# Pre-norm attention layer (delta-rule RNN) with ReLU FFN on 8 cores: four sets of eight PSUM copies each become one VectorE instruction

## The reference

```
q = silu(x @ Wq); k = silu(x @ Wk); v = silu(x @ Wv)
f = x @ Wf1 @ Wf2; log_f = log_sigmoid(f)
beta = sigmoid(x @ Wbeta) * 2.0
k = l2norm(k); k_ = -beta * k
gk = interleave(log_f, 0); a = interleave(k_ * exp(log_f), k_); bb = interleave(k, k)
kk = interleave(0, k); vv = interleave(0, v); qq = interleave(0, q)
def step(S, inp):
    bS = b_t @ S
    S = exp(g) * S + a_t (x) bS + k_t (x) v_t
    o = q_t @ S
y = o[odd steps] * sigmoid(x @ Wog1 @ Wog2)
y = y / sqrt(mean(y*y over the head) + EPS) * norm_w
attn = y @ Wo
x = x + attn(layernorm(x))
x = x + (relu(layernorm(x) @ w1 + b1) @ w2 + b2)
```

## Time and profile before

| | us |
|---|---|
| median of 2 runs of the kernel before | 6550.92 (6539.94 and 6561.9) |
| the profiled execution, its own time | 6540.92 |
| its span (first to last instruction, slowest core) | 6539.3 |
| spans of the eight cores | 6481.3 to 6539.3 |

### The profile page before, as it was taken

One profiled execution on the slowest core, in us unless ns is written; L12 is line 12 of the kernel. 1 busy time (PEld: TensorE's weight loads), 2 busy tenths in 40 slices (PEclk: granted clock), 3 DMA queues, 4 the chain that ended last, 5 costly groups with the idle time before them and its releaser, 6 DMA issues.

```text
span 6539.3 us, 88394 instructions; the slowest of 8 cores (6481.3 to 6539.3 us)
## 1 busy us (share of the span) xinstructions
PE 4050.7 (62%) x30717; PEld 2720.6 (42%) x30797; DVE 2399.2 (37%) x5555; ACT 1899.4 (29%) x3443; POOL 458.3 (7%) x456
## 2 busy tenths in 40 slices
PE   0066566665656565666565666656565648788888
PEld 0034344443434343434343433434353425555555
DVE  0144435353535353534344343435353511111111
ACT  0042333233332323232323233333323212222222
POOL 0010101010100000010101010101000000000000
PEclk9976666676766676676766666666666768888898
DMA  9511010101010101010110101010101030000000
GB/s 106 123 46 42 24 46 20 46 20 46 20 65 1 65 1 65 1 65 7 59 33 33 46 20 46 20 46 20 62 4 46 1 126 33 30 27 27 27 27 26
DMA packets 92522, 255.96 MB, mean 39 GB/s; under 512 B 11531, under 2 KB 14252, under 8 KB 89270
## 3 DMA queue, kind: packets, MB, share of 16 engines
q1 hardware_dynamic: 91382, 229.33, 10.4%
q0 software_dynamic: 704, 20.97, 2.9%
HBM read 233.48 MB, written 58.72 MB: 45 GB/s over the span
## 4 chain that ended last, share of the span: by engine, by line
PE 48%; DVE 20%; ACT 11%; issue 9%; DMA 6%; another core or an unknown queue 3%; POOL 2%; SPq 1%; DVEq 1%; ACTq 0%; POOLq 0%
PE PB L84 48%; DVE Pm_sb L84 6%; DVE X_sb L84 3%; DVE Lam L84 2%; ACT U_sb L84 2%; DVE lncol L84 2%; DMA Wbuf<-wbf_Wk 2%; ACT v_bf L84 1%; DVE yT_bf L84 1%; ACT L84 1%; SPq L84 1%; DVE scrA L84 1%; DMA x_sb<-x2scratch 1%; ACT yT_bf L84 1%
## 5 line engine op out<-in xcount | busy, mean ns | idle before, releaser
L84 ACT CAST U_sb<-PB 128x512 bf16<-128x512 f32 x1024 | 600.0, 586 | 1387.3 <-PE PB L84 1347.3
L84 DVE CAST X_sb<-PB 128x512 bf16<-128x512 f32 x640 | 439.2, 686 | 639.5 <-PE PB L84 639.5
L84 PE MATMUL PB<-U_sb,consts 128*128 128x128 bf16 x3584 | 597.3, 253 | 104.8 <-ACT U_sb L84 104.8
L84 PE MATMUL PB<-U_sb,Pm_sb 128*128 128x128 bf16 x3584 | 591.1, 254 | 42.9 <-DVE Pm_sb L84 40.7
L84 DVE CAST Pm_sb<-PB 128x512 bf16<-128x512 f32 x768 | 518.8, 683 | 172.3 <-PE PB L84 172.3
L84 PE MATMUL PB<-consts,yT_bf 128*128 128x128 bf16 x640 | 76.5, 294 | 709.0 <-DVE yT_bf L84 638.1
L84 PE MATMUL PB<-X_sb,Pm_sb 128*128 128x128 bf16 x2048 | 220.9, 237 | 416.9 <-DVE Pm_sb L84 416.9
L84 PEld LDWEIGHTS PB<-U_sb,consts 128*128 128x128 bf16 x3584 | 412.7, 115 | 134.9 <-issue 125.3
L84 PE MATMUL PB<-W_bf,hfm 128*128 128x512 bf16 x2000 | 443.1, 381 | 17.7 <-ACT hfm L84 15.9
L84 PEld LDWEIGHTS PB<-U_sb,Pm_sb 128*128 128x128 bf16 x3584 | 414.1, 116 | 64.0 <-issue 61.5
L84 PEld LDWEIGHTS PB<-consts,yT_bf 128*128 128x128 bf16 x640 | 58.4, 132 | 727.6 <-issue 727.6
(11 more groups left out here) (142 smaller groups left out, 6858.8 us busy)
## 6 DMA issues: line engine op xcount, KB each, us to landing
Wbuf<-wbf_Wv SPq DMA_DIRECT2D x128, 256.0 KB, 7.5
Wbuf<-wbf_Wo SPq DMA_DIRECT2D x128, 256.0 KB, 4.7
Wbuf<-wbf_Wq SPq DMA_DIRECT2D x15, 2048.0 KB, 7.9
Wbuf<-wbf_Wk SPq DMA_DIRECT2D x120, 256.0 KB, 5.9
wbf_w<-w POOLq DMA_DIRECT2D x2, 8192.0 KB, 81.5
x_sb<-x SPq DMA_DIRECT2D x32, 512.0 KB, 3.9
x2scratch<-x_sb SPq DMA_DIRECT2D x32, 512.0 KB, 2.9
W_bf<-wbf_w SPq DMA_DIRECT2D x64, 256.0 KB, 5.7
```

The costliest lines, as they stand in the source:

```text
L84: inst = getattr(e, fname)(*args, **kw)
```

## The change

In three places the eight copies of `pe_transpose_8` become one `tensor_copy` of 128x1024 (64x1024 for Ktm): Atm, Ktm, and lnT in phase A, where a permuted access pattern (`_perm_in`, `_perm_out`) orders the eight blocks. The eight multiplications by nw_col ahead of Wo become one `tensor_tensor` with nw_col broadcast. Phase B's copies stay as they are. The lists that are dealt into the levels get 14 instructions shorter (32, nper = 5).

```
 def pe_transpose_8(src_fn, dst_fn, tsrc, tdst, pbank, tpbank, n=8,
-                   rows=128):
+                   rows=128, dst_batched=None):
...
+    if dst_batched is not None:
+        out_ap, in_ap = dst_batched
+        b.op("V", "tensor_copy", out_ap, in_ap,
+             reads=[tpbank], writes=[tdst])
+        return
...
+def _perm_in(pbank):
+    return pbank[:].bitcast(BF16).rearrange(
+        "p (s k e) -> p k s e", s=2, k=4)
+def _perm_out(dst, grp):
+    return dst[:, grp * 1024:(grp + 1) * 1024].rearrange(
+        "p (k s e) -> p k s e", k=4, s=2)
...
-                    lambda i: lnT[:, idx[i][0] * MACRO + idx[i][1] * 128:
-                                  idx[i][0] * MACRO + (idx[i][1] + 1) * 128],
-                    tyT, tlnT, pbank, tpbank)
+                    None, tyT, tlnT, pbank, tpbank,
+                    dst_batched=(_perm_out(lnT, grp), _perm_in(pbank)))
...
-                            lambda i: Atm[:, i * 128:(i + 1) * 128],
-                            tAm, tAtm, pb, tpb)
+                            None, tAm, tAtm, pb, tpb,
+                            dst_batched=(Atm[:], pb[:].bitcast(BF16)))
...
-                            lambda i: Ktm[:, i * 128:(i + 1) * 128],
-                            tKt, tKtm, pb2, tpb2, rows=64)
+                            None, tKt, tKtm, pb2, tpb2, rows=64,
+                            dst_batched=(Ktm[:], pb2[:].bitcast(BF16)[0:64, :]))
...
-                        for i in range(8):
-                            kk, sub = idx[i]
-                            b.op("V", "tensor_scalar_mul",
-                                 q_bf[:, kk * MACRO + sub * 128:
-                                      kk * MACRO + (sub + 1) * 128],
-                                 pbank[:].bitcast(BF16)[:, i * 128:(i + 1) * 128],
-                                 nw_col[:, kk:kk + 1],
-                                 reads=[tpbank, tnw], writes=[tq], inc=(i == 7))
...
+                        nw4 = nwb[:, grp * 4:(grp + 1) * 4]
+                        nw_b = nw4.rearrange("p (k o) -> p k o", o=1)
+                        nw_b = nw_b.unsqueeze(2).broadcast_to((128, 4, 2, 128)) \
...
+                        b.op("V", "tensor_tensor", _perm_out(q_bf, grp),
+                             _perm_in(pbank), nw_b, ALU.mult,
+                             reads=[tpbank, tnw], writes=[tq])
```

More of the change, by code:

```diff
@@ L968, in build_program @@
                                  inc=(i == 7))
-                        for i in range(8):
-                            kk, sub = idx[i]
-                            b.op("V", "tensor_scalar_mul",
-                                 q_bf[:, kk * MACRO + sub * 128:
-                                      kk * MACRO + (sub + 1) * 128],
-                                 pbank[:].bitcast(BF16)[:, i * 128:(i + 1) * 128],
-                                 nw_col[:, kk:kk + 1],
-                                 reads=[tpbank, tnw], writes=[tq], inc=(i == 7))
+                        nwb = bass.AP(nw_col.handle if hasattr(nw_col, "handle")
+                                      else nw_col, 0, [[8, 128], [1, 8]]) \
+                            if False else nw_col[:]
+                        nw4 = nwb[:, grp * 4:(grp + 1) * 4]
+                        nw_b = nw4.rearrange("p (k o) -> p k o", o=1)
+                        nw_b = nw_b.unsqueeze(2).broadcast_to((128, 4, 2, 128)) \
+                            if hasattr(nw_b, "unsqueeze") else nw_b
+                        b.op("V", "tensor_tensor", _perm_out(q_bf, grp),
+                             _perm_in(pbank), nw_b, ALU.mult,
+                             reads=[tpbank, tnw], writes=[tq])
                     for sub in range(NSUB):
```

## The result

| | us |
|---|---|
| before, median of 10 runs | 6539.0 (6519.75 to 6607.27) |
| changed kernel, median of 11 runs | 6643.6 (6632.97 to 6775.05) |
| ratio | 1.0154, 95% interval 1.0118 to 1.0189 |

The account below looks back on a forecast made before the run. Waits between engines, in a closed DVE-PE ring of doubling levels, were taken to bound the kernel. From 6540.9 us, +120 for the 48 chunks with a next one and -31 for the gains made 6630 us, range 6560 to 6690.

Parts of the forecast that it names:

- The moved wait: Level 2: PE queues behind a transpose waiting for the second Am product; 1.66 us more at full clock, 3.15 at half.
- Which clock: Level 2 after the new wait: PE at half clock in nine levels of ten, making 3.0 us a chunk.
- Level 3: Five transposes in front instead of one: idle falls from 2.4 to about 1.8 us, gain 0.5 us a chunk.
- levels 3 and 4 became slower: Sign of a wrong forecast; level 3 was expected near 1.8 us and level 4 to change by 0.
- The batched copies: A batched copy takes 0.68 us, q_bf 1225 ns; lnT gains 15 us in all, q_bf 13 us.
- The small term of chunk 0: Atm and Ktm copies ahead of T_sb in chunk 0: 0.2 us each time, 3 us in all, bounds 0 and 15.
- The hidden copies: Atm and Ktm copies in chunks 1 to 3 fall into DVE's idle stretch, hidden by PE and casts; gain 0.
- The sum: 6540.9 + 120 - 31 = 6630 us, 1.4% more than the profiled execution, 1.2% above the median of the two runs shown.
- Gains alone: Rival: the Am wait costs nothing, so 6510 us, perhaps 6490 with level 3; chance 0.06.
- the slow batch: Rival: the batched copy takes 1.22 us in place of 0.68, giving 6650 us; chance 0.07.
- full clock at the wait: Rival: PE at full clock in level 2 behind the Am wait, giving 6566 us; chance 0.10.
- slow clock throughout: Rival: half clock through levels 2 to 4 of 48 chunks, up to 4.9 us a chunk, 6747 us; chance 0.09.

Follow-up runs that it names:

- f3: The changed kernel with 34 filler products on PE ahead of the transpose that waits for Am in level 2; 6661.9 us, ratio 1.0126 to the kernel before.
- a2: Eight copies each as in the kernel before, but dealt to the levels as in the changed kernel; 6745.4 us, ratio 1.0308.
- a3: Changed kernel with Am products still behind level 1's casts, but the first transpose one level later; 6527.7 us, ratio 1.0008 to the kernel before.
- b1: Changed kernel's batched copies, list dealt 7, 7, 7, 7, 4, so Am products stand early and seven transposes precede level 2; 6538.9 us, ratio 0.9992.
- f1: b1 plus filler products nobody reads on PE, making up seven instructions with the transposes ahead of levels 1 to 4; 6374.2 us, ratio 0.9755.
- f4: f1 plus 24 fillers ahead of the HQ products, 4 ahead of levels 5 and 6, 10 ahead of the output products; 6284.9 us, ratio 0.9485.

## Why the prediction was right, point by point

**The sign and the size.** 6630 us was forecast and 6643.6 measured; against the kernel before of the same runs that is +1.5% where +1.2 to 1.4% was said.

**The moved wait** was right in mechanism and size. Worked out were 4.90 us between the casts at half clock and 3.41 at full clock; 4.85 was measured (f3, mostly at full clock: 3.66). Am ended 1.39 us behind the cast where 1.40 was said. a2 has the order without the batching and the loss, a3 has the late Am without the waiting transpose and no loss: the cause is the transpose queued on PE ahead of work that is ready.

**Which clock.** Nine in ten at half clock were taken; it was all of them (19 of 6144 U products of level 2 ran at full clock). This made the term 48 x 3.1 = 148 us in place of 144.

**Level 3** is the term that was wrong. The prediction gave it 0.5 us a chunk for its five transposes ("if five transposes do what seven do"), 24 us in all. Measured was 2.36 us, 0.1 more than before, with 0.52 of these levels at half clock where 0.36 were. That "levels 3 and 4 became slower" was one of the prediction's own signs of being wrong, and both did, by 0.1 us each (level 4 from 2.04 to 2.12). f3 shows what was missing: with the same five transposes, but PE busy through the wait of level 2, level 3 took 1.86 us. What PE had done before counts too, not only the transposes right in front. In level 3 those in front make no visible difference: six of them (b1) give 2.21 us, one of them (before) 2.26.

**The batched copies** were right: 683 to 692 ns (0.68), 1225 ns (1.225), lnT 0.91 us a macro tile (0.92), q_bf 0.84 (0.82). The small term of chunk 0 (0.2 us) was wrong: T_sb starts 0.3 us earlier, but nothing behind it does, so it is worth nothing.

**The hidden copies** were costed at nothing, and their DVE time was indeed hidden. Not seen was the tail: the changed deal puts five transposes ahead of level 5 and one ahead of level 6, where three and none stood, and the tail is 0.3 us shorter in each of the three chunks. The copies are not the cause, since a2, which has the same places and eight copies each, has 8.51 us too; in all deals without fillers the tail goes with the transposes ahead of levels 5 and 6 (8.5 to 8.6 us with five and one, 8.9 with three and none, 9.2 with none). The time is saved in the output products behind level 6 (5.5 us from the first to the last in place of 5.8); level 6's own U products were at full clock before too. f1 has 8.62 us with none of these transposes, so here as well what PE did earlier counts.

**The sum.** In the traces: level 2 +148 us (144 forecast), the other levels +13 (-24), the tail -16 (0), lnT and q_bf -28 (-28), chunk 0 nothing (-3): 117 us, where the forecast had 89. The two terms of the clock's kind were off by 37 and by 16 us and cancelled in part; that the total came out as close is to that extent luck.

**The rivals.** Gains alone was refuted by PE's wait for Am; the slow batch by the 683 ns; full clock at the wait by the traces (none of the U products of level 2); slow clock throughout by levels 3 and 4, which came to 2.36 and 2.12 and not to 2.97 us.

## What to carry to other kernels

When instructions are dealt into a pipeline by count, making the list shorter moves every one of them: look at what stands first in each slot, and never put an instruction that waits in front of independent work on an in-order engine. A merge of small copies is worth only what someone waits for, here two places of four. And before tuning the order, look at what TensorE did in the microseconds ahead of each burst: idle work there can be worth more (5% here) than the instructions saved.

## What the runs showed that I had not expected

Moving transposes that cost nobody any time changes the time of the products behind them, by 0.4 us in level 2 (1.76 us with seven in front, 2.18 with one). In this chain with many short idle times PE did the U products of a third of the levels 1 and 3 at 1.2 GHz, and nearly all at 2.4 GHz once fillers stood in the idle times (f1). Filler products in the idle times raised the slowest core's granted clock over the span from 0.736 to 0.816 (f4), and took 5% off the time. Phase B, where PE is busy for 80% of the time at a granted clock of 0.87 (kernel before, 5300 to 6500 us), had no fillers; whether they would pay there was not tried. How many fillers are needed at the least was not tried either.
